# Regrouping a gather's 128 rows as 32 samples by 4 fields, and collecting all results for one turn at the end of a factorization-machine kernel

## The chip, the cores and the metric

The kernel runs on one core of a Trainium2 chip. The metric is the device time of that core in microseconds (us). Each core has TensorE (PE, matmul), VectorE (DVE), ScalarE (ACT), GpSimd (POOL), SyncE (SP), which here only issues transfers, and 16 DMA engines that move data between HBM and the on-chip memories SBUF and PSUM, both of 128 partitions.

## The reference, cut to what matters

For 2048 samples with 32 fields each, every field has its own table of 1250 rows of 496 floats. A sample picks one row of every table; the rows are scaled by the sample's values, and a factorization-machine term and a small hidden layer give one number per sample.

```python
gathered = jax.vmap(lambda table, idx: table[idx], in_axes=(0, 1), out_axes=1)(emb, xi)
e = gathered * xv[:, :, None]                  # 2048 x 32 x 496
s = jnp.sum(e, axis=1)
qi = 0.5 * (s * s - jnp.sum(e * e, axis=1))
h = jax.nn.relu(xv @ W1 + b1)                  # 2048 x 1024
x = jnp.concatenate([qi, h], axis=1)
return x @ W2 + b2                             # 2048 x 1
```

All data are float32. The gathered rows are 2048 x 32 x 1984 bytes, 130 MB.

## The kernel before, in words

**Tiling.** The samples go in 16 blocks of 128. A block is 8 quads, a quad is 4 gathers, and a gather is one indirect DMA that POOL issues: it brings 128 rows, one for each partition, from the addresses in one column of `index_rows` in SBUF (line 142). There are 16 x 8 x 4 = 512 gathers. The buffer `gathered` holds the 8 quads of one block, so quad s of block i goes where quad s of block i-1 was.

**Before**, the 128 partitions of a gather are 4 samples by 32 fields.

**For each quad**, in a stream that runs over all blocks: ACT squares the rows of two gathers at a time into PSUM (`squares`, line 160); DVE multiplies each of the four squared tiles by the weights `w2_all` and sums along the row (line 271, with a sum output into `norms`); PE multiplies the gathered rows by `weights`, a matrix that holds the samples' values in the right columns, and adds them up over the 8 quads in `sum_ps` (line 189). In quad 2 of a block PE also computes the hidden layer (line 202), which DVE weighs after quad 4 (line 283). After quad 3, DVE fills `weights` for the next block (line 233).

**At a block's end** ACT squares the sums (`sum_squared`, line 166), and DVE scales the norms by the squared values (line 288), spreads them over the samples' columns (line 293), weighs the squared sums (line 300), adds three partial results (line 305); PE adds the spread norms over partitions (line 176), and DVE adds that to the rest, after quad 1 of the next block (`finish`, line 241). After the last block PE turns the 128 x 16 results with an identity matrix (line 209), DVE copies them out of PSUM (line 310) and SP stores them.

**What sets the order.** Each engine works through its own list in the order written, and waits on semaphores. POOL waits ahead of each quad from block 1 on, until ACT has squared and PE has summed what the quad's buffer held (`squared`, `summed`). Row addresses are computed by DVE from the raw indices (`rows_of`, lines 222, 224 and 227), first for block 0 alone, then for the other 15 blocks together while the first gathers are issued.

Of the kernel before, what the change touches and what calls it, by code (L numbers as in the profile page):

```python
# [5 lines left out]
ALU = mybir.AluOpType  # L6
# [4 lines left out]
P = 128  # L11
# [4 lines left out]
def fm_kernel(nc, index, value, value_t, emb, w1, b1, w2, b2, out):  # L16


    fields, batch = value_t.shape
# [3 lines left out]
    per = P // fields  # L23
    blocks = batch // P
    quads = P // (GROUPS * per)
# [5 lines left out]
    assert per * quads == COLS and gathers == blocks * in_block and dim <= 512  # L31

    with ExitStack() as ctx:  # L33
# [11 lines left out]
        index_rows = sb("index_rows", [P, gathers], I32)  # L45
        values = sb("values", [P, 2, gathers])
        first_row = sb("first_row", [P, 1])
        last_row = sb("last_row", [P, 1])
        own_row = sb("own_row", [P, per])
        ones = sb("ones", [P, 1])  # L50

        weights = sb("weights", [P, 2, quads, GROUPS, COLS])
        gathered = sb("gathered", [P, quads, GROUPS, dim])

        weighted = sb("weighted", [P, GROUPS + halves + 1, 512])
        w2_all = sb("w2_all", [P, dim + hidden])
        w1_b1 = sb("w1_b1", [fields + 1, hidden])
        value_rows = sb("value_rows", [fields + 1, batch])
        sum_squared = sb("sum_squared", [P, 512])

        norms = sb("norms", [P, quads, GROUPS])
        norms_scaled = sb("norms_scaled", [P, quads, GROUPS])
        norms_spread = sb("norms_spread", [P, GROUPS, quads, per])
        parts = sb("parts", [P, 2 + halves])
        partial = sb("partial", [P, 1])
        y = sb("y", [P, blocks])

        column_less_row = sb("column_less_row", [P, P])
        identity = sb("identity", [P, P])
        y_rows = sb("y_rows", [blocks, P])  # L70
# [5 lines left out]
        norm_ps = psum("norm_ps", [P, 512])  # L76
# [19 lines left out]
        scaled = sem("scaled")  # L96
        spread_ready = sem("spread_ready")
        norm_ready = sem("norm_ready")
        partial_ready = sem("partial_ready")
        y_ready = sem("y_ready")  # L100
        identity_ready = sem("identity_ready")
        y_turned = sem("y_turned")
        y_rows_ready = sem("y_rows_ready")
# [5 lines left out]
        def _(sp):  # L109
# [6 lines left out]
            sp.dma_start(parts[:, 1 + halves:], b2.to_broadcast([P, 1])).then_inc(w2_loaded, 16)  # L116

            sp.wait_ge(y_rows_ready, 1)
            sp.dma_start(out.rearrange("(c p) o -> c (p o)", p=P), y_rows[:]).then_inc(stored, 16)
# [3 lines left out]
        def _(pool):  # L123
            for b in range(per):
                nc.gpsimd.iota(first_row[b * fields:(b + 1) * fields, :], [[0, 1]], base=0,
                               channel_multiplier=vocab,
                               allow_small_or_imprecise_dtypes=True).then_inc(rows_known, 1)
            pool.wait_ge(rows_known, per)
            nc.gpsimd.iota(column_less_row[:], [[1, P]], base=0, channel_multiplier=-1,
                           allow_small_or_imprecise_dtypes=True).then_inc(rows_known, 1)  # L130
            for i in range(blocks):
# [16 lines left out]
        def _(act):  # L148
            act.dma_start(w1_b1[0:fields, :], w1).then_inc(w1_loaded, 16)
            act.dma_start(w1_b1[fields:fields + 1, :], b1).then_inc(w1_loaded, 16)  # L150
            act.dma_start(value_rows[0:fields, :], value_t).then_inc(w1_loaded, 16)
            for i in range(blocks):
                for s in range(quads):
                    for half in range(pairs):
                        pair = slice(pairs * half, pairs * half + pairs)
                        act.wait_ge(fetched[s][half], (i + 1) * pair_arrived)
                        if i + s > 0:

                            act.wait_ge(normed, (i * quads + s - 1) * GROUPS + pairs * (half + 1))
# [4 lines left out]
                if i > 0:  # L164
                    act.wait_ge(sum_squared_used, i)
# [178 lines left out]
```

## Time and profile before

| | |
|---|---|
| time, median of 3 runs | 659.15 us (658.28 to 659.45) |
| the profiled execution, its own time | 656.74 us |
| its span, first to last instruction | 654.9 us |
| POOL busy | 485.8 us, 74% |
| DVE busy | 384.4 us, 59% |
| PE busy | 308.0 us, 47% |
| ACT busy | 265.8 us, 41% |
| data moved | 132.08 MB, mean 202 GB/s |

Busy time is the time in which an engine ran instructions. POOL's instructions here are the gathers: an entry is the time that POOL spends on issuing one, and between two entries there is always a gap that the profile calls "issue", in which nothing that it sees is waited for. In a timeline row the first number is the start from the span's start, the second how long it took, and the brackets tell how long the engine had been idle and for what. A DVE operation with a sum output shows a second entry for reading the sum (DVE_READ_ACCUMULATOR). DVE overlaps the end of one operation with the start of the next, so the next one can start some 0.08 us before the reported end.

### The profile page before, as it was taken

Reading aid. Unit: us, or ns where it says so; the run is one execution under the profiler, and the core shown is the slowest. Engines: PE = TensorE matmul, PEld = TensorE weight load, DVE = VectorE, ACT = ScalarE, POOL = GpSimd, SP = SyncE. Lnnn points to the kernel's source line nnn. Section 1 sums busy time; section 2 is a strip of 40 time slices with the busy share of each in tenths; the row PEclk is TensorE's granted clock in tenths of the full one; section 3 lists DMA queues with packets and bytes.
Section 4 is the critical chain, followed back from the end, with each engine's and each line's share of the span. In section 5 each row is a group of like instructions: output and inputs, shape, how many; then the busy total and the mean of one; then the engine's idle time right before and its main releaser. Section 6 shows DMA issues by size and latency. Waiting matters only on the chain.

```text
span 654.9 us, 4973 instructions
## 1 busy us (share of the span) xinstructions
PE 308.0 (47%) x1122; PEld 55.9 (9%) x1122; DVE 384.4 (59%) x1330; ACT 265.8 (41%) x273; POOL 485.8 (74%) x521
## 2 busy tenths in 40 slices
PE   1544536354453643546346353453635445364354
PEld 0101001010010100101001010100101001010010
DVE  6556655656666465655556555665555665556554
ACT  2344444434443434344343434444344444343433
POOL 5777777777777777777777777777777777777773
DMA  7777777777777777777777777777777777777774
GB/s 218 203 205 203 203 205 204 203 203 203 203 204 204 203 204 202 207 201 204 204 203 205 204 203 203 203 206 204 203 204 202 204 203 205 205 203 202 204 202 114
DMA packets 33647, 132.08 MB, mean 202 GB/s; under 512 B 8577, under 2 KB 8721, under 8 KB 33586
## 3 DMA queue, kind: packets, MB, share of 16 engines
q0 software_dynamic: 32768, 130.06, 72.4%
q1 hardware_dynamic: 752, 1.31, 0.7%
q10 hardware_dynamic: 98, 0.40, 0.2%
q8 instruction: 9, 0.15, 0.1%
q14 instruction: 20, 0.16, 0.1%
HBM read 131.72 MB, written 0.01 MB: 201 GB/s over the span
## 4 chain that ended last, share of the span: by engine, by line
POOL 60%; issue 20%; PE 10%; DMA 8%; DVE 1%; POOLq 0%; ACT 0%; DVEq 0%
POOL gathered L142 60%; DMA gathered<-emb,index_rows 7%; PE sum_ps L189 6%; PE hidden_ps L202 5%; DMA index_raw<-index 0%; POOLq L139 0%; DVE weighted L271 0%; POOLq L33 0%; ACT squares L160 0%; DVE weighted L300 0%; PE norm_ps L209 0%; DVE index_rows L227 0%; DVE y_rows L310 0%; DVE index_wrap L224 0%; DVE norms_scaled L288 0%
## 5 line engine op out<-in xcount | busy, mean ns | idle before, releaser
L142 POOL DMA_INDIRECT gathered<-emb,index_rows x512 | 484.8, 947 | 158.8 <-issue 151.1
L271 DVE SCALAR_TENSOR_TENSOR weighted<-squares,w_all 128x496 f32<-128x496 f32 x512 | 324.6, 672 | 261.3 <-ACT squares L160 261.0
L160 ACT ACTIVATE squares<-gathered 128x992 f32<-128x992 f32 x256 | 256.3, 1001 | 366.2 <-DMA gathered<-emb,index_rows 343.1
L189 PE MATMUL sum_ps<-gathered,weights 128*32 128x496 f32 x1024 | 240.8, 1031 | 343.4 <-DMA gathered<-emb,index_rows 343.4
L189 PEld LDWEIGHTS sum_ps<-gathered,weights 128*32 128x32 f32 x1024 | 29.0, 140 | 526.8 <-issue 526.8
L202 PE MATMUL hidden_ps<-w_b,value_rows 33*128 33x512 f32 x64 | 60.5, 1097 | 0.0
L271 DVE DVE_READ_ACCUMULATOR weighted<-squares,w_all 128x1 f32 x512 | 42.4, 83 | 0.0
L202 PEld LDWEIGHTS hidden_ps<-w_b,value_rows 33*128 33x128 f32 x64 | 18.6, 321 | 42.4 <-issue 42.4
L283 DVE SCALAR_TENSOR_TENSOR weighted<-hidden_ps,w_all 128x512 f32<-128x512 f32 x32 | 20.7, 686 | 0.0
L166 ACT ACTIVATE sum_squared<-sum_ps 128x496 f32<-128x496 f32 x16 | 9.3, 583 | 16.8 <-PE sum_ps L189 16.8
L233 DVE TENSOR_TENSOR weights<-values,own_row 128x16 f32<-128x16 f32 x128 | 12.7, 170 | 0.0
L300 DVE SCALAR_TENSOR_TENSOR weighted<-sum_squared,w_all 128x496 f32<-128x496 f32 x16 | 10.7, 666 | 0.0
L176 PEld LDWEIGHTS norm_ps<-ones,norms_spread 128*128 128x128 f32 x32 | 8.0, 313 | 26.8 <-issue 24.2
L176 PE MATMUL norm_ps<-ones,norms_spread 128*128 128x1 f32 x32 | 9.4, 363 | 0.9 <-DVE norms_spread L293 0.9
L293 DVE TENSOR_TENSOR norms_spread<-norms_scaled,own_row 128x128 f32<-128x128 f32 x16 | 4.8, 298 | 0.5
L288 DVE TENSOR_TENSOR norms_scaled<-norms,values 128x32 f32<-128x32 f32 x16 | 3.1, 192 | 0.6
L305 DVE TENSOR_REDUCE partial<-parts 128x1 f32<-128x4 f32 x16 | 2.5, 157 | 0.6
L283 DVE DVE_READ_ACCUMULATOR weighted<-hidden_ps,w_all 128x1 f32 x32 | 2.7, 83 | 0.0
L241 DVE TENSOR_TENSOR y<-partial,norm_ps 128x1 f32<-128x1 f32 x16 | 2.4, 151 | 0.0
L160 ACT ACT_TABLE_LOAD x1 | 1.3, 1283 | 2.1 <-issue 2.1
L263 DVE MEMSET value_rows<- 1x2048 f32 x1 | 1.8, 1765 | 0.5 <-ACT squares L160 0.5
L248 DVE MEMSET weights<- 128x2048 f32 x1 | 1.8, 1765 | 0.4 <-issue 0.4
(19 smaller groups left out, 7.3 us busy)
## 6 DMA issues: line engine op xcount, KB each, us to landing
gathered<-emb,index_rows POOLq DMA_INDIRECT x512, 3.7
w_all<-w SPq DMA_DIRECT2D x1, 760.0 KB, 6.1
values<-value SPq DMA_DIRECT2D x1, 256.0 KB, 3.5
value_rows<-value_t ACTq DMA_DIRECT2D x1, 256.0 KB
index_raw<-index SPq DMA_DIRECT2D x1, 240.0 KB, 4.7
w_b<-w ACTq DMA_DIRECT2D x1, 128.0 KB
index_raw<-index SPq DMA_DIRECT2D x1, 16.0 KB, 3.0
w_b<-b ACTq DMA_DIRECT2D x1, 4.0 KB
```

What stands on the lines that cost most here:

```text
L142: nc.gpsimd.indirect_dma_start(out=gathered[:, s, j, :], out_offset=None, in_=emb, in_offset=bass.IndirectOffsetOnAxis(ap=index_rows[:, g: ...
L160: nc.scalar.activation(squares[:, pair, 0:dim], gathered[:, s, pair], ACT.Square).then_inc(squared, 1)
L166: nc.scalar.activation(sum_squared[:, 0:dim], sum_ps[:, 0:dim], ACT.Square).then_inc(sum_squared_ready, 1)
L176: nc.tensor.matmul(norm_ps[:, 0:1], norms_spread[:], ones[:], start=True, stop=True).then_inc(norm_ready, 1)
L189: last = nc.tensor.matmul(sum_ps[j * COLS:(j + 1) * COLS, 0:dim], weights[:, i % 2, s, j, :], gathered[:, s, j, :], start=(s == 0), stop=( ...
L202: last = nc.tensor.matmul(hidden_ps[:, h, :], value_rows[:, i * P:(i + 1) * P], w1_b1[:, h * 512:(h + 1) * 512], start=True, stop=True)
L233: last = nc.vector.tensor_tensor(weights[:, i % 2, s, :, s * per:(s + 1) * per], values[:, 0, at].unsqueeze(2).to_broadcast([P, GROUPS, per]),
L271: nc.vector.scalar_tensor_tensor(weighted[:, j, 0:dim], squares[:, j, 0:dim], -0.5, w2_all[:, 0:dim], ALU.mult, ALU.mult, accum_out=norms[ ...
L283: nc.vector.scalar_tensor_tensor(weighted[:, GROUPS + h, :], hidden_ps[:, h, :], 0.0, w2_all[:, dim + h * 512:dim + (h + 1) * 512], ALU.ma ...
L288: nc.vector.tensor_tensor(norms_scaled[:].rearrange("p s j -> p (s j)"), norms[:].rearrange("p s j -> p (s j)"), values[:, 1, i * in_block ...
L293: nc.vector.tensor_tensor(norms_spread[:], norms_scaled[:].rearrange("p s j -> p j s").unsqueeze(3).to_broadcast([P, GROUPS, quads, per]), ...
L300: nc.vector.scalar_tensor_tensor(weighted[:, GROUPS + halves, 0:dim], sum_squared[:, 0:dim], 0.5, w2_all[:, 0:dim], ALU.mult, ALU.mult, ac ...
```

## The change

- A gather holds 32 samples by 4 fields in place of 4 samples by 32 fields. The weights of PE's matmul are then a mask of 32 columns times the values, filled by one DVE operation for each block; the mask is kept in PSUM (`y_ps`, columns 128 to 159).
- The norms are multiplied by the values at once: line 271's constant -0.5 becomes a scalar read from `values` for each partition (line 305 of the new kernel). The scaling, the spreading, the partial sum and the per-block matmul go away.
- The results of all blocks are kept (`norms`, `hidden_part`, `sum_part`) and turned at the very end by three matmuls with a 0/1 mask (`add_lines`).
- The weighing of the squared sums moves from a block's end to after quad 1 of the next block (`weigh_sums`), ACT's squaring of the sums to after quad 0 of the next block (`square_sums`), and the two halves of the hidden layer are weighed by one operation.
- `normed` is counted once a quad, `summed` once in two quads. POOL waits once in two quads, on `summed` alone; PE waits on `squared` in place of the transfers themselves, save in the last quad, so that `summed` implies both.
- The row addresses are computed with constants and a 128 x 32 table of first rows, and the 128 x 2048 memset of `weights` goes away.

The core of the diff:

```diff
-            for b in range(per):
-                nc.gpsimd.iota(first_row[b * fields:(b + 1) * fields, :], [[0, 1]], base=0,
-                               channel_multiplier=vocab,
+            for f in range(per):
+                nc.gpsimd.iota(first_row[f * COLS:(f + 1) * COLS, :], [[per * vocab, quads], [0, GROUPS]],
+                               base=f * vocab, channel_multiplier=0,
                                allow_small_or_imprecise_dtypes=True).then_inc(rows_known, 1)
...
-                    if i > 0:
-
-                        pool.wait_ge(squared, ((i - 1) * quads + s + 1) * pairs)
-                        pool.wait_ge(summed, (i - 1) * quads + s + 1)
+                    if i > 0 and s % freed == 0:
+
+                        pool.wait_ge(summed, (i - 1) * in_summed + s // freed + 1)
...
+            def square_sums(i):
+                act.wait_ge(summed, (i + 1) * in_summed)
+                if i > 0:
+                    act.wait_ge(sum_squared_used, i)
+                nc.scalar.activation(sum_squared[:], sum_ps[:, 0:dim],
+                                     ACT.Square).then_inc(sum_squared_ready, 1)
...
+                    if i + s > 0:
+
+                        act.wait_ge(normed, i * quads + s)
...
-                        if i + s > 0:
-
-                            act.wait_ge(normed, (i * quads + s - 1) * GROUPS + pairs * (half + 1))
...
+                    if s == 0 and i > 0:
+                        square_sums(i - 1)
+            square_sums(blocks - 1)
...
-                    for half in range(pairs):
-                        pe.wait_ge(fetched[s][half], (i + 1) * pair_arrived)
+                    if i == blocks - 1 and s == quads - 1:
+                        for half in range(pairs):
+                            pe.wait_ge(fetched[s][half], (i + 1) * pair_arrived)
+                    else:
+
+                        pe.wait_ge(squared, (i * quads + s + 1) * pairs)
...
+            def add_lines(part, first, last):
+
+                return nc.tensor.matmul(y_ps[0:lines, 0:COLS], part[:].rearrange("p i j -> p (i j)"),
+                                        own_sample[:], start=first, stop=last)
...
             def refill_weights(i):
-                for s in range(quads):
-                    at = slice(i * in_block + s * GROUPS, i * in_block + (s + 1) * GROUPS)
-                    last = nc.vector.tensor_tensor(
-                        weights[:, i % 2, s, :, s * per:(s + 1) * per],
-                        values[:, 0, at].unsqueeze(2).to_broadcast([P, GROUPS, per]),
-                        own_row[:].unsqueeze(1).to_broadcast([P, GROUPS, per]), ALU.mult)
-                last.then_inc(weights_ready, 1)
...
+                nc.vector.scalar_tensor_tensor(
+                    weights[:, i % 2],
+                    values[:, 0, i * in_block:(i + 1) * in_block].unsqueeze(2).to_broadcast(
+                        [P, in_block, COLS]), 1.0,
+                    y_ps[:, P:P + COLS].unsqueeze(1).to_broadcast([P, in_block, COLS]),
+                    ALU.mult, ALU.mult).then_inc(weights_ready, 1)
+
+            def weigh_sums(i):
+                dve.wait_ge(sum_squared_ready, i + 1)
+                nc.vector.scalar_tensor_tensor(
+                    weighted[:, GROUPS], sum_squared[:], 0.5, w2_all[:, 0:dim], ALU.mult, ALU.mult,
+                    accum_out=sum_part[:, i:i + 1]).then_inc(sum_squared_used, 1)
...
-                        nc.vector.scalar_tensor_tensor(
-                            weighted[:, j, 0:dim], squares[:, j, 0:dim], -0.5, w2_all[:, 0:dim],
-                            ALU.mult, ALU.mult, accum_out=norms[:, s, j:j + 1]).then_inc(normed, 1)
+                        last = nc.vector.scalar_tensor_tensor(
+                            weighted[:, j], squares[:, j, 0:dim], values[:, 1, g:g + 1],
+                            w2_all[:, 0:dim], ALU.mult, ALU.mult,
+                            accum_out=norms[:, i, s, j:j + 1])
+                    last.then_inc(normed, 1)
                     if s == 1 and i > 0:
-                        finish(i - 1)
+                        weigh_sums(i - 1)
...
+            add_quads(blocks - 1, blocks).then_inc(norm_lines_ready, 1)
+            weigh_sums(blocks - 1)
+            dve.wait_ge(sum_squared_used, blocks)
+            by_line(sum_part, sum_lines, blocks - 1, blocks).then_inc(sum_lines_ready, 1)
+            dve.wait_ge(y_summed, 1)
+            nc.vector.tensor_scalar(y[:], y_ps[0:lines, 0:COLS], b2_all[0:lines, :], None, ALU.add
+                                    ).then_inc(y_ready, 1)
```

How the change moves instructions is seen in each engine's list. A row gives the line, the operation, what it writes and reads, its shape and what it waits for; "x7" is seven such in a row.

On DVE, at quads 0 and 1 of block 1, the list of before has the addition of `finish` (line 241) behind the last squared tile of quad 1:

```order
L271 SCALAR_TENSOR_TENSOR weighted,norms<-squares,w_all 128x496 [waits squared]
L271 SCALAR_TENSOR_TENSOR weighted,norms<-squares,w_all 128x496
L241 TENSOR_TENSOR y<-partial,norm_ps 128x1 [waits norm_ready]
L271 SCALAR_TENSOR_TENSOR weighted,norms<-squares,w_all 128x496 [waits squared]
L271 SCALAR_TENSOR_TENSOR weighted,norms<-squares,w_all 128x496
```

The changed kernel has at the same place:

```order
L305 SCALAR_TENSOR_TENSOR weighted,norms<-squares,values,w_all 128x496 [waits squared]
L305 SCALAR_TENSOR_TENSOR weighted,norms<-squares,values,w_all 128x496
L262 SCALAR_TENSOR_TENSOR weighted,sum_part<-sum_squared,w_all 128x496 [waits sum_squared_ready]
L305 SCALAR_TENSOR_TENSOR weighted,norms<-squares,values,w_all 128x496 [waits squared]
L305 SCALAR_TENSOR_TENSOR weighted,norms<-squares,values,w_all 128x496
```

A small addition has been replaced by the weighing of 496 squared sums, which reads `sum_squared` and `w2_all`, both in SBUF.

On POOL, the list of before from the first row tables to the first quads of block 1 is:

```order
L125 IOTA first_row 32x1 x4
L129 IOTA column_less_row 128x128 [waits rows_known]
L142 DMA gathered<-emb,index_rows 128x496 [waits index_ready]
L142 DMA gathered<-emb,index_rows 128x496 x31
L142 DMA gathered<-emb,index_rows 128x496 [waits summed,squared,index_ready]
L142 DMA gathered<-emb,index_rows 128x496 x3
L142 DMA gathered<-emb,index_rows 128x496 [waits summed,squared]
```

The changed kernel's POOL list there is:

```order
L132 IOTA first_row 32x32 x4
L137 IOTA column_less_row 32x32 [waits rows_known]
L137 IOTA column_less_row 32x32 x3
L150 DMA gathered<-emb,index_rows 128x496 [waits index_ready]
L150 DMA gathered<-emb,index_rows 128x496 x31
L150 DMA gathered<-emb,index_rows 128x496 [waits summed,index_ready]
L150 DMA gathered<-emb,index_rows 128x496 x7
L150 DMA gathered<-emb,index_rows 128x496 [waits summed]
```

The number of gathers is the same; a wait stands ahead of every eighth instead of every fourth, and is for one semaphore.

On DVE, the list of before begins with the address operations and the fills of `weights`:

```order
L222 TENSOR_SCALAR index_wrap<-index_raw 128x32 [waits first_loaded,setup]
L224 SCALAR_TENSOR_TENSOR index_wrap<-index_wrap,first_row,index_raw 128x32 [waits setup]
L227 TENSOR_SCALAR index_rows<-index_wrap,first_row,last_row 128x32 [waits setup]
L248 MEMSET weights 128x2048
...
L233 TENSOR_TENSOR weights<-values,own_row 128x4x4 [waits values_loaded,setup]
L233 TENSOR_TENSOR weights<-values,own_row 128x4x4 x7
L256 TENSOR_TENSOR values<-values 128x512
L222 TENSOR_SCALAR index_wrap<-index_raw 128x480 [waits index_loaded,setup]
L224 SCALAR_TENSOR_TENSOR index_wrap<-index_wrap,first_row,index_raw 128x480 [waits setup]
L227 TENSOR_SCALAR index_rows<-index_wrap,first_row,last_row 128x480 [waits setup]
```

The changed kernel's list begins so:

```order
L241 TENSOR_SCALAR index_wrap<-index_raw 128x32 [waits first_loaded,rows_known]
L243 SCALAR_TENSOR_TENSOR index_wrap<-index_raw,index_wrap 128x32 [waits setup]
L246 SCALAR_TENSOR_TENSOR index_rows<-index_wrap,first_row 128x32 [waits setup]
L282 TENSOR_SCALAR own_sample<-column_less_row 128x32 [waits rows_known]
L283 TENSOR_SCALAR y_ps<-column_less_row 128x32
L253 SCALAR_TENSOR_TENSOR weights<-values,y_ps 128x1024 [waits values_loaded,setup]
L287 SCALAR_TENSOR_TENSOR values<-values 128x512
L241 TENSOR_SCALAR index_wrap<-index_raw 128x480 [waits index_loaded,setup]
L243 SCALAR_TENSOR_TENSOR index_wrap<-index_raw,index_wrap 128x480 [waits setup]
L246 SCALAR_TENSOR_TENSOR index_rows<-index_wrap,first_row 128x480 [waits setup]
```

The memset and the eight small fills have given way to two comparisons and one fill of 1024 elements; of the three address operations the third reads two tensors now.

## Rows read from the trace of the kernel before

**Rows 1.** The page: busy shares, and the costliest group of instructions.

```profile
PE 308.0 (47%) x1122; PEld 55.9 (9%) x1122; DVE 384.4 (59%) x1330; ACT 265.8 (41%) x273; POOL 485.8 (74%) x521
...
L142 POOL DMA_INDIRECT gathered<-emb,index_rows x512 | 484.8, 947 | 158.8 <-issue 151.1
```

**Rows 2.** Timeline of DVE and POOL at the start.

```profile
4.09 0.25 DVE L224 SCALAR_TENSOR_TENSOR index_wrap<-index_wrap,first_row,index_raw 128x32 f32<-128x32 f32 x1
4.38 0.30 DVE L227 TENSOR_SCALAR index_rows<-index_wrap,first_row,last_row 128x32 int32<-128x32 f32 x1
4.97 1.09 POOL L142 DMA_INDIRECT gathered<-emb,index_rows  x1 [3.12 <-DVE index_rows L227]
...
8.00 0.68 DVE L256 TENSOR_TENSOR values<-values 128x512 f32<-128x512 f32 x1
8.72 0.41 DVE L222 TENSOR_SCALAR index_wrap<-index_raw 128x480 f32<-128x480 int32 x1
8.87 1.08 POOL L142 DMA_INDIRECT gathered<-emb,index_rows  x1 [0.30 <-issue]
...
10.25 1.01 POOL L142 DMA_INDIRECT gathered<-emb,index_rows  x1 [0.30 <-issue]
```

**Rows 3.** Timeline: the last gather, and what ACT and DVE do last.

```profile
644.51 0.95 POOL L142 DMA_INDIRECT gathered<-emb,index_rows  x1 [0.30 <-issue]
...
650.29 0.58 ACT L166 ACTIVATE sum_squared<-sum_ps 128x496 f32<-128x496 f32 x1 [1.05 <-PE sum_ps L189]
...
651.02 0.67 DVE L300 SCALAR_TENSOR_TENSOR weighted<-sum_squared,w_all 128x496 f32<-128x496 f32 x1
...
651.73 0.16 DVE L305 TENSOR_REDUCE partial<-parts 128x1 f32<-128x4 f32 x1
651.92 0.15 DVE L241 TENSOR_TENSOR y<-partial,norm_ps 128x1 f32<-128x1 f32 x1
...
652.84 0.28 DVE L310 COPY y_rows<-norm_ps 16x128 f32<-16x128 f32 x1 [0.77 <-PE norm_ps L209]
```

**Rows 4.** Waits on POOL, 10.2 to 45 us: us in total, times, longest.

```profile
POOL gathered L142 <- issue: 8.5, 28, 0.3
```

**Rows 5.** Waits on POOL, 45 to 640 us.

```profile
POOL gathered L142 <- issue: 140.7, 462, 0.3
POOL gathered L142 <- PE sum_ps L189: 4.6, 15, 0.3
```

**Rows 6.** Timeline of DVE and POOL, late in block 11 to 12.

```profile
490.34 0.67 DVE L271 SCALAR_TENSOR_TENSOR weighted<-squares,w_all 128x496 f32<-128x496 f32 x1
...
490.71 0.95 POOL L142 DMA_INDIRECT gathered<-emb,index_rows  x1 [0.30 <-PE sum_ps L189]
...
491.48 0.67 DVE L300 SCALAR_TENSOR_TENSOR weighted<-sum_squared,w_all 128x496 f32<-128x496 f32 x1
491.97 1.00 POOL L142 DMA_INDIRECT gathered<-emb,index_rows  x1 [0.30 <-issue]
```

**Rows 7.** Timeline of DVE and POOL at the end of another block.

```profile
130.38 0.29 DVE L293 TENSOR_TENSOR norms_spread<-norms_scaled,own_row 128x128 f32<-128x128 f32 x1
130.44 1.04 POOL L142 DMA_INDIRECT gathered<-emb,index_rows  x1 [0.30 <-issue]
```

**Rows 8.** Timeline of DVE and POOL at the end of a third block.

```profile
411.38 0.67 DVE L300 SCALAR_TENSOR_TENSOR weighted<-sum_squared,w_all 128x496 f32<-128x496 f32 x1
411.94 0.95 POOL L142 DMA_INDIRECT gathered<-emb,index_rows  x1 [0.30 <-issue]
```

**Rows 9.** Groups of DVE by line, whole span: busy, mean ns of one.

```profile
L288 DVE TENSOR_TENSOR norms_scaled<-norms,values 128x32 f32<-128x32 f32 x16 | 3.1, 192 | 0.6
```

**Rows 10.** Timeline: the first of the 15 `finish` additions between blocks.

```profile
60.02 0.15 DVE L241 TENSOR_TENSOR y<-partial,norm_ps 128x1 f32<-128x1 f32 x1
60.35 0.95 POOL L142 DMA_INDIRECT gathered<-emb,index_rows  x1 [0.30 <-issue]
```

**Rows 11.** Timeline: the fourteenth of them.

```profile
580.55 0.15 DVE L241 TENSOR_TENSOR y<-partial,norm_ps 128x1 f32<-128x1 f32 x1
...
580.76 0.95 POOL L142 DMA_INDIRECT gathered<-emb,index_rows  x1 [0.30 <-issue]
```

**Rows 12.** Line 142, whole span: from a gather's issue to its landing.

```profile
DMA to landing us min/median/max: 3.4/3.7/5.5
```

More of the change, by code:

```diff
@@ L22, in fm_kernel @@
     hidden = w1.shape[1]
[L23 removed]
+    per = P // COLS
     blocks = batch // P
[L25 removed]
+    quads = fields // per
     gathers = index.shape[1]
@@ L30, in fm_kernel @@
     pair_arrived = 16 * GROUPS // pairs
-    assert per * quads == COLS and gathers == blocks * in_block and dim <= 512
+    freed = 2
+    in_summed = quads // freed
+    lines = blocks * GROUPS
+    assert per * quads == fields and gathers == blocks * in_block and dim <= 512
+    assert lines <= P and halves == 2
     with ExitStack() as ctx:
@@ L219, in step, with rows_of @@
                 dve.wait_ge(setup, done[0])
-            def rows_of(columns):
+            def rows_of(first, last):
+                columns = slice(first * in_block, last * in_block)
+                by_block = [P, last - first, in_block]
                 step(nc.vector.tensor_scalar(index_wrap[:, columns], index_raw[:, columns], 0.0,
@@ new lines, in by_line, with add_quads @@
+            def by_line(part, lines_of, first, last):
+                count = [P, last - first, GROUPS]
+                return nc.vector.tensor_tensor(
+                    lines_of[:, first:last], part[:, first:last].unsqueeze(2).to_broadcast(count),
+                    own_group[:].unsqueeze(1).to_broadcast(count), ALU.mult)
+            def add_quads(first, last):
+                return nc.vector.tensor_reduce(
+                    norm_lines[:, first:last], norms[:, first:last].rearrange("p i s j -> p i j s"),
+                    mybir.AxisListType.X, ALU.add)
@@ L244, in _ @@
             dve.wait_ge(rows_known, per)
-            step(nc.vector.tensor_scalar(last_row[:], first_row[:], float(vocab - 1), None, ALU.add))
             dve.wait_ge(first_loaded, 16)
-            rows_of(slice(0, in_block))
-            nc.vector.memset(weights[:], 0.0)
-            nc.vector.memset(ones[:], 1.0)
-            step(nc.vector.memset(own_row[:], 0.0))
-            for b in range(per):
-                last = nc.vector.memset(own_row[b * fields:(b + 1) * fields, b:b + 1], 1.0)
@@ L257, in _ @@
             dve.wait_ge(index_loaded, 16)
-            rows_of(slice(in_block, gathers))
-            dve.wait_ge(rows_known, per + 1)
-            nc.vector.tensor_scalar(identity[:], column_less_row[:], 0.0, None, ALU.is_equal
-                                    ).then_inc(identity_ready, 1)
+            rows_of(1, blocks)
+            step(nc.vector.memset(own_group[:], 0.0))
+            for j in range(GROUPS):
+                last = nc.vector.memset(own_group[j * COLS:(j + 1) * COLS, j:j + 1], 1.0)
@@ L262, in _ @@
+            step(last)
             dve.wait_ge(w1_loaded, 48)
@@ new lines, in _ @@
+                    if i == blocks - 1 and s == 5:
+                        dve.wait_ge(hidden_used, blocks)
+                        by_line(hidden_part, hidden_lines, 0, blocks).then_inc(hidden_lines_ready, 1)
+                        dve.wait_ge(sum_squared_used, blocks - 1)
+                        by_line(sum_part, sum_lines, 0, blocks - 1)
+                        dve.wait_ge(normed, (blocks - 1) * quads)
+                        add_quads(0, blocks - 1)
+            dve.wait_ge(normed, blocks * quads)
```

159 lines of the change are left out of this document (65 added, 94 removed).

## The prediction, as put on record

> **What bounds the kernel now.** I read the page first. POOL is the busiest engine, and all of it is one group: 512 gathers of 947 ns, with 151 us of "issue" gaps between them [rows 1]. One gather so costs 0.95 + 0.30 = 1.25 us from start to start. From the first start at 4.97 us [rows 2] to the last at 644.51 us [rows 3] there are 511 steps in 639.5 us, 1.2516 us each. The list of POOL's waits shows that it never waits for anybody in earnest: the 28 gathers of block 0 that have no buffer to wait for had 8.5 us of gaps, 0.304 us each [rows 4]; later 462 gaps total 140.7 us, 0.305 us each, and the 15 that the profile lays to PE total 4.6 us, 0.307 us each [rows 5]. So the kernel is a metronome of 512 beats, with 5 us ahead of it and 654.9 - 644.5 = 10.4 us behind the last beat. An engine other than POOL matters only if it makes POOL miss a beat, or in those two ends. 0.2% is 1.3 us, or 2.6 ns a beat.
>
> What can disturb a beat shows in the timeline. A beat's entry is 0.95 us long almost always. At 491.97 it is 1.00, and a DVE operation that reads two SBUF tensors (line 300, `sum_squared` and `w2_all`) had started at 491.48 and was still running, its reported end 0.18 us past the beat's start [rows 6]. At 130.44 it is 1.04: line 293, also with two SBUF inputs, ends 0.23 us past the start [rows 7]. At 8.87 it is 1.08: line 222 ends 0.26 us past it; it reads one tensor, but two elements at a time (480 in 0.41 us, against 0.68 us for line 256's 512) [rows 2]. At 411.94 it is the usual 0.95 with line 300 ending 0.11 us past it [rows 8]. All four fit one rule: **a beat that begins while such an operation runs is late by the operation's reported end minus the beat's start minus 0.13 us** (0.05, 0.10, 0.13 and 0). Line 271, which reads one tensor in PSUM and one in SBUF, runs across a beat's start 243 times, as at 490.34 to 491.01 over the start at 490.71, and delays none: 0.95 [rows 6]. Late beats are never made up, as POOL has no slack.
>
> The Trainium skill (SBUF — State Buffer, "Who interferes with whom") says that a DVE instruction with two SBUF inputs shares a read interface with a GpSimd instruction that reads SBUF, and that the second to come blocks until the first is done. The trace agrees in kind; its four delays are shorter, by 0.13 us, than the operation's remaining time. The same page ("A bandwidth-pool intuition that's wrong") reports blocking until DVE's end and some 115 ns more; by that, term c below would be 13 x 0.245 = 3.2 us more (an estimate from that page), and the trace's 1.00 in place of some 1.25 at 491.97 speaks against it.
>
> **The change part by part.**
>
> a) *Waits on POOL.* Before, 120 pairs of waits; after, 60 single ones. Gaps with and without waits differ by 0.001 to 0.003 us [rows 4, 5], so 60 to 180 waits removed are worth from nothing to 180 x 0.003 = 0.5 us. I take 0: the gaps are alike within the rounding. The new wait comes later, for PE's second quad of a pair, which itself waits for ACT. Quad 1 of block 1 is issued by 55 us, landed by 59 us, squared by 60 us and summed by 62 us, and POOL asks for it ahead of beat 64, at 4.97 + 64 x 1.2516 = 85 us. 20 us of cover; cost 0. If that cover were gone, all that stands behind POOL's wait, which is every later gather, would slip.
>
> b) *Start.* The first beat follows the third address operation. Lines 224 and 227 take 0.25 and 0.30 us, each with per-partition scalars as well as tensors [rows 2]. Their replacements have no such scalar; the nearest row is a two-input operation of the same 32 elements, 0.19 us [rows 9]. That is 0.06 + 0.11 = **-0.17**; bounds 0 and -0.2. POOL's iotas grow but are done before the indices land. Next come collisions: before, the beats at 8.87 and 10.25 lost 0.13 and 0.06 us [rows 2]. After, `values` is squared and the addresses of 15 blocks computed some 2 us sooner, and three operations of the latter's kind have two SBUF inputs, each about 0.7 us (line 256, 0.68 us [rows 2]). They fill 2.0 of some 3 us, so one or two beats start under one and lose between 0 and 0.68 - 0.13 = 0.55 us each: 0 to 1.1 us, I take 0.5, net of before **+0.3**.
>
> c) *The weighing of the squared sums*, 0.67 us with two SBUF inputs. Before, at a block's end, it happened to start mostly just behind a beat. After, it starts where line 241 starts now, right behind the last tile of quad 1, 15 times. That place is 0.33 us ahead of a beat the first time [rows 10] and 0.21 us the fourteenth [rows 11]; over the 15 the distances are 0.33, 0.26, 0.96, 0.33, 0.25, 0.55, 0.37, 0.27, 0.37, 0.32, 0.50, 0.40, 0.26, 0.21 and 1.01 us. An operation of 0.67 us that starts d ahead of a beat delays it by 0.67 - d - 0.13 = 0.54 - d. Summed over the twelve where it is positive: **2.6 us**. The chain to this place is tied to the beat: landing 3.7 us behind the issue [rows 12], 1.0 us of ACT, two DVE operations. The only thing that moves it is those two operations, which gain a per-partition scalar. No row prices that for them: at most the 0.25 - 0.19 = 0.06 us by which line 224 exceeds line 288 [rows 2, 9], at least nothing, as starts of DVE operations overlap. Two such shift the place by 0 to 0.12 us toward the beat, which gives 2.6 to 4.2 us over the 15. I take the middle, 0.06 us later: **+3.4**.
>
> d) *Collisions removed.* Lines 293 and 300 go from the block's end. Four beats lost 0.31 us there in all, the largest two of them in [rows 6, 7] (0.05 and 0.10), the others 0.08 each: **-0.3**. The eight fills of line 233 cost no beat today; their one successor reads only one SBUF tensor, and hides behind the beats.
>
> e) *Steady work of DVE, ACT and PE.* DVE is 59% busy [rows 1] and loses more than it gains; ACT now waits for a whole quad to be weighed: 1.0 us of ACT and four times 0.6 us of DVE is 3.5 us for a quad, against four beats, 5.0 us. **0.** Without that slack every quad would cost the difference.
>
> f) *Tail.* The sums are ready on ACT at 650.87, the weighing starts at 651.02 behind lines 288 and 293 [rows 3]; after, one short reduction stands there, and it starts at about 650.93: -0.09. Behind it, a reduction and an addition (651.73 and 651.92) become one operation: -0.19. The matmul stays; the copy of 128 elements (0.28 us) becomes one of 32: -0.08. The store goes out as 64 pieces of 128 bytes in place of 16 of 512: from 0 to, at most, what is saved; I take +0.1. Sum **-0.26**.
>
> Sum: -0.17 + 0.3 + 3.4 - 0.3 - 0.26 = **+3.0 us** on the profiled execution's 656.74. The median of the runs is 659.15; the same gives **662.1 us**, +0.45%. What a measurement of this kernel can tell from no change is 0.2%, 1.3 us.
>
> **The rivals.**
>
> 1. *Not slower.* The sum operation lies clear of the beats: if the new arrangement of rows makes transfers land 0.2 us sooner, it ends before the beat, and if some 0.35 us later, it starts behind one. Then c is near 0 and the rest is -0.17 + 0.3 - 0.3 - 0.26 = -0.4: 658.7 us, no change. For it: landings scatter from 3.4 to 5.5 us [rows 12], two of the 15 places lie clear already. Against: thirteen of 15 distances are 0.21 to 0.55 us, so the median is stable, and the rows are as long and as scattered as before. It decides where c is below 1.7 us, which a place 0.1 us farther ahead of the beat gives (1.5 us). Chance 0.22.
>
> 2. *Faster.* As 1, with the start's collisions also missed and the waits worth their 0.5 us: -0.17 - 0.2 - 0.3 - 0.26 - 0.5 = -1.4 us, 657.7 us. All the small savings must come in together. Chance 0.07.
>
> 3. *Full blocking.* Each of the 13 beats under 0.67 us away waits for the operation's whole rest, 0.13 us more: +1.7, 663.8 us. The four rows above speak against it, but they are short overlaps. Chance 0.12.
>
> 4. *The per-partition scalar makes line 305 block POOL as well.* It is read from SBUF like `w2_all`. By the rule above, applied to each run of line 271 across a beat, that is 62 us: 721 us. Against it: nothing in the trace tells, since the scalar operations there have two tensors anyway or stand alone. Chance 0.03. The Trainium skill (DVE: scalar operands, raw-bit mode, write accounting and state across instructions, "Scalar operands") says that such a scalar does not take up the second tensor stream, which no run here shows yet.
>
> **How the numbers follow.** The forecast, c between 1.5 and 5 us, has 0.56, its own range 660.3 to 663.6. With the rivals 1, 2, 3 and 4 (0.22, 0.07, 0.12, 0.03) that is one. Slower by over 0.2%: 0.56 + 0.12 + 0.03, less a little for the forecast's low edge, 0.68; same 0.24; faster 0.08. The range from 658.5 to 664.3 leaves out rival 4, rival 2 and the edges of 1 and 3.
>
> **What would show it.** In the changed kernel's timeline: 512 beats of 0.95 us, gap 0.30 with and without waits (a); first beat at 4.80 us (b); in 10 to 14 of the 15 blocks one beat of 1.1 to 1.4 us, with line 262 started 0.1 to 0.5 us before it (c); no long beats elsewhere but at the start (d), and none under line 305 (rival 4); from the last beat to the end 10.1 us in place of 10.4 (f). I am wrong if line 262 runs across beats that stay at 0.95 us, if it starts elsewhere in the beat, or if the steady gap itself has changed by some ns.

## The result and the profile after

The changed kernel took 661.28 us (median of 7 runs, 661.20 to 661.48), the kernel before 658.61 us on the same chip (7 runs, the first three included). The ratio is 1.0038 (95% interval 1.0026 to 1.0049): 2.7 us slower, clear of the 0.2% that this measurement can tell. The forecast was 3.0 us.

The page of the changed kernel has, against [rows 1]:

```profile
PE 300.4 (46%) x1094; PEld 45.7 (7%) x1094; DVE 410.0 (62%) x1125; ACT 265.8 (40%) x273; POOL 491.5 (75%) x524
...
L150 POOL DMA_INDIRECT gathered<-emb,index_rows x512 | 489.9, 957 | 157.6 <-issue 155.8
L305 DVE SCALAR_TENSOR_TENSOR weighted<-squares,values,w_all 128x496 f32<-128x496 f32 x512 | 355.5, 732 | 242.0 <-ACT squares L176 241.6
```

POOL still sets the pace. Its 512 gathers are busy 5.1 us longer in sum (484.8 in rows 1, 489.9 here) with the same gaps. DVE's tile operation grew from 672 to 732 ns; what is new in it is the per-partition scalar (the third experiment takes it away again).

The timeline of the changed kernel's DVE and POOL where the squared sums of block 0 are weighed, against [rows 10] (start, duration, idle time before; a "beat" is one gather's issue, as in the prediction):

```profile
59.09 0.73 DVE L305 SCALAR_TENSOR_TENSOR weighted<-squares,values,w_all 128x496 f32<-128x496 f32 x1
...
59.75 0.67 DVE L262 SCALAR_TENSOR_TENSOR weighted<-sum_squared,w_all 128x496 f32<-128x496 f32 x1
...
60.01 1.23 POOL L150 DMA_INDIRECT gathered<-emb,index_rows  x1 [0.30 <-issue]
...
61.54 0.95 POOL L150 DMA_INDIRECT gathered<-emb,index_rows  x1 [0.30 <-issue]
```

Line 262 starts 0.26 us ahead of the beat at 60.01 and its reported end is 0.41 us past it; the beat takes 1.23 in place of 0.95 us: 0.41 - 0.13 = 0.28. The next beat follows 1.53 us behind. Line 305, which runs across the beats beside it, leaves them at 0.95. Three other blocks, in which the distance differs:

```profile
222.54 0.67 DVE L262 SCALAR_TENSOR_TENSOR weighted<-sum_squared,w_all 128x496 f32<-128x496 f32 x1
...
223.02 1.02 POOL L150 DMA_INDIRECT gathered<-emb,index_rows  x1 [0.30 <-issue]
...
303.04 0.67 DVE L262 SCALAR_TENSOR_TENSOR weighted<-sum_squared,w_all 128x496 f32<-128x496 f32 x1
...
303.65 0.94 POOL L150 DMA_INDIRECT gathered<-emb,index_rows  x1 [0.30 <-issue]
...
624.91 0.67 DVE L262 SCALAR_TENSOR_TENSOR weighted<-sum_squared,w_all 128x496 f32<-128x496 f32 x1
...
625.06 1.35 POOL L150 DMA_INDIRECT gathered<-emb,index_rows  x1 [0.30 <-issue]
```

At 0.48 us of distance the beat loses 0.07 us, at 0.61 nothing, at 0.15 us 0.40. Of the 15 places 14 have such a late beat; their start-to-start times exceed 1.25 us by 3.93 us together, and each by its operation's reported end minus the beat's start minus 0.13 us, to 0.01 us.

The start of the changed kernel, against [rows 2]:

```profile
3.75 0.19 DVE L243 SCALAR_TENSOR_TENSOR index_wrap<-index_raw,index_wrap 128x32 f32<-128x32 int32 x1
3.97 0.19 DVE L246 SCALAR_TENSOR_TENSOR index_rows<-index_wrap,first_row 128x32 int32<-128x32 f32 x1
...
4.44 1.10 POOL L150 DMA_INDIRECT gathered<-emb,index_rows  x1 [1.79 <-DVE index_rows L246]
...
5.53 0.68 DVE L287 SCALAR_TENSOR_TENSOR values<-values 128x512 f32<-128x512 f32 x1
5.84 1.19 POOL L150 DMA_INDIRECT gathered<-emb,index_rows  x1 [0.30 <-issue]
```

From the second address operation to the first beat it is 0.69 us in place of 0.88 (4.09 to 4.97): 0.19 us saved, with operations of 0.19 us each. One beat, at 5.84, starts under an operation with two SBUF tensors and takes 0.24 us more.

The tail, against [rows 3]:

```profile
649.28 0.95 POOL L150 DMA_INDIRECT gathered<-emb,index_rows  x1 [0.31 <-issue]
...
655.05 0.58 ACT L165 ACTIVATE sum_squared<-sum_ps 128x496 f32<-128x496 f32 x1 [1.05 <-PE sum_ps L198]
...
655.67 0.68 DVE L262 SCALAR_TENSOR_TENSOR weighted<-sum_squared,w_all 128x496 f32<-128x496 f32 x1
...
656.38 0.16 DVE L269 TENSOR_TENSOR sum_lines<-sum_part,own_group 128x4 f32<-128x4 f32 x1
...
657.06 0.24 DVE L338 TENSOR_SCALAR y<-y_ps,b_all 64x32 f32<-64x32 f32 x1 [0.52 <-PE y_ps L218]
657.33 0.53 SPq L126 DMA_DIRECT2D out<-y  x1
```

The last beat starts 10.16 us ahead of the span's end (10.2 by the rounded 659.4), against 10.41 before.

**A part of the two traces' difference is not the change's.** The spans differ by 4.5 us, the medians by 2.7. The changed kernel's profile is of an execution at its median (661.24), that of before one of 656.74, 1.9 us under the median of before (658.61). The beats that nothing disturbs (start to start below 1.27 us) average 1.2503 us before and 1.2535 us after; 494 of them make 1.6 us. The first and the fifth run below settle whose that is.

### The profile page after: what moved, and what is told of

Its sections match the earlier page's. It is cut to its first block, busy times and chain, and to the rows that moved or that the text cites. A ratio compares the mean times of both kernels' runs of the same rounds, so it can differ in the third digit from the quotient of the medians.

```text
span 659.4 us, 4310 instructions
## 1 busy us (share of the span) xinstructions
PE 300.4 (46%) x1094; PEld 45.7 (7%) x1094; DVE 410.0 (62%) x1125; ACT 265.8 (40%) x273; POOL 491.5 (75%) x524
## 4 chain that ended last, share of the span: by engine, by line
POOL 74%; issue 24%; DMA 1%; DVE 1%; POOLq 0%; ACT 0%; PE 0%; DVEq 0%
POOL gathered L150 74%; DMA gathered<-emb,index_rows 1%; DMA index_raw<-index 0%; DVE weighted L305 0%; POOLq L39 0%; ACT squares L176 0%; DVE weighted L262 0%; PE y_ps L218 0%; DVE y L338 0%; DVE norm_lines L274 0%; DVE index_rows L246 0%; DVE index_wrap L243 0%; DVE index_wrap L241 0%; DVE sum_lines L269 0%; DVEq L279 0%
## 5 line engine op out<-in xcount | busy, mean ns | idle before, releaser
L150 POOL DMA_INDIRECT gathered<-emb,index_rows x512 | 489.9, 957 | 157.6 <-issue 155.8
L305 DVE SCALAR_TENSOR_TENSOR weighted<-squares,values,w_all 128x496 f32<-128x496 f32 x512 | 355.5, 732 | 242.0 <-ACT squares L176 241.6
L198 PEld LDWEIGHTS sum_ps<-gathered,weights 128*32 128x32 f32 x1024 | 26.2, 140 | 566.1 <-ACT squares L176 468.8
L305 DVE DVE_READ_ACCUMULATOR weighted<-squares,values,w_all 128x1 f32 x512 | 42.5, 83 | 0.0
L319 DVE SCALAR_TENSOR_TENSOR weighted_hidden<-hidden_ps,w_all 128x1024 f32<-128x1024 f32 x16 | 19.5, 1220 | 0.0
L253 DVE SCALAR_TENSOR_TENSOR weights<-values,y_ps 128x1024 f32<-128x1024 f32 x16 | 19.5, 1217 | 0.0
```

The source lines that it names most:

```text
L150: nc.gpsimd.indirect_dma_start(out=gathered[:, s, j, :], out_offset=None, in_=emb, in_offset=bass.IndirectOffsetOnAxis(ap=index_rows[:, g: ...
L198: last = nc.tensor.matmul(sum_ps[j * COLS:(j + 1) * COLS, 0:dim], weights[:, i % 2, s * GROUPS + j, :], gathered[:, s, j, :], start=(s == ...
L253: nc.vector.scalar_tensor_tensor(weights[:, i % 2], values[:, 0, i * in_block:(i + 1) * in_block].unsqueeze(2).to_broadcast([P, in_block, ...
L305: last = nc.vector.scalar_tensor_tensor(weighted[:, j], squares[:, j, 0:dim], values[:, 1, g:g + 1], w2_all[:, 0:dim], ALU.mult, ALU.mult, ...
L319: nc.vector.scalar_tensor_tensor(weighted_hidden[:], hidden_ps[:], 0.0, w2_all[:, dim:].rearrange("p (h c) -> p h c", h=halves), ALU.max, ...
```

## The experiments

Each ratio is to the kernel before, run beside it on the same chip; its 95% interval stands in brackets. Before took 656.79 us (19 runs) beside the first four kernels and 657.33 us (14 runs) beside the others. The theory is the prediction's: a beat that starts while DVE runs an operation with two SBUF tensors is late, and the change puts one such operation ahead of a beat in each block. The rivals are that the time comes from the regrouped rows, from the waits, or from another feature of the place behind quad 1.

**Before again**, no edit.

> The kernel before, once more, for its profile. The first trace of before had an undisturbed beat (start to start of two gathers) of 1.2503 us, the changed kernel's 1.2535 us, 1.6 us over 494 beats. If that difference is one execution against another, this profile shows a beat of 1.2530 to 1.2540 us and a span near 657 us; if it comes from the change (the regrouped rows, the waits), it shows 1.2500 to 1.2506 us again.

It took 657.06 us, span 655.2. The undisturbed beat was 1.2503 us, as in the first trace. That left the changed kernel's 1.2535 open, which the fifth run took up. It also showed a rarer collision at the old place, here in the timeline of DVE and POOL:

```profile
210.29 0.67 DVE L300 SCALAR_TENSOR_TENSOR weighted<-sum_squared,w_all 128x496 f32<-128x496 f32 x1
210.33 1.45 POOL L142 DMA_INDIRECT gathered<-emb,index_rows  x1 [0.30 <-issue]
```

Line 300 began 0.04 us ahead of a beat, so its end is 0.63 us past it, and the beat is 0.50 us too long: the same rule at the longest overlap of a late beat in any trace here. The same trace shows where the rule ends, at another block:

```profile
611.22 0.72 DVE L300 SCALAR_TENSOR_TENSOR weighted<-sum_squared,w_all 128x496 f32<-128x496 f32 x1
611.24 0.95 POOL L142 DMA_INDIRECT gathered<-emb,index_rows  x1 [0.30 <-issue]
```

Here line 300 began 0.02 us ahead of the beat. By the rule the beat would be late by 0.57 us; it is on time, and it is DVE's operation that is longer, 0.72 us in place of 0.67. The traces have eleven beats of this kind, behind operations with two SBUF tensors that began 0.00 to 0.04 us ahead of them; every late beat has a lead of 0.04 us or more. In this execution lines 293 and 300 took 0.85 us from the beats, against 0.31 in the first trace. The kernel before is not free of the effect; it mostly just misses it.

**The sums in PSUM.** The operation stays, at its place and in its order, and has one SBUF input in place of two.

```diff
-                nc.scalar.activation(sum_squared[:], sum_ps[:, 0:dim],
+                nc.scalar.activation(sum_ps[:, 0:dim], sum_ps[:, 0:dim],
...
-                    weighted[:, GROUPS], sum_squared[:], 0.5, w2_all[:, 0:dim], ALU.mult, ALU.mult,
+                    weighted[:, GROUPS], sum_ps[:, 0:dim], 0.5, w2_all[:, 0:dim], ALU.mult, ALU.mult,
...
-                        pe.wait_ge(sum_squared_ready, i)
+                        pe.wait_ge(sum_squared_used, i)
```

> The changed kernel, but ACT squares the sums in place in PSUM, and line 262 reads them there: at the same place in the same order, with one SBUF tensor in place of two. Theory (beats that start under a two-SBUF operation are late): the 14 long beats of 1.02 to 1.35 us go away, 3.9 us less, 657.4 us, 0.998 of before. Rival (the time comes from the regrouped rows or from what else is on DVE at that place): the beats stay long and the time stays at 661.3 us, 1.004 of before.

655.73 us, ratio 0.998 (0.997 to 0.999): faster than both kernels. The timeline at the same place of block 1:

```profile
59.81 0.67 DVE L262 SCALAR_TENSOR_TENSOR weighted<-sum_ps,w_all 128x496 f32<-128x496 f32 x1
60.11 0.95 POOL L150 DMA_INDIRECT gathered<-emb,index_rows  x1 [0.31 <-issue]
```

Line 262 starts 0.30 us ahead of the beat (0.26 us in the changed kernel), is as long as there, and the beat is 0.95 us. No beat after the second is late in the whole execution, though in all 15 blocks line 262 starts 0.14 to 0.45 us ahead of one. So it is the second SBUF input, and not the place, its length or what is near it. The undisturbed beat is 1.2501 us, with the regrouped rows and the new waits.

**The constant in place of the per-partition scalar** (this leaves out the scaling of the norms by the values).

```diff
-                            weighted[:, j], squares[:, j, 0:dim], values[:, 1, g:g + 1],
+                            weighted[:, j], squares[:, j, 0:dim], -0.5,
```

> The changed kernel with the constant -0.5 in line 305 in place of the per-partition scalar, so the norms are left unscaled by the values. Each tile's operation should be 0.67 us long again in place of 0.73, and the place of the weighing lies 0.12 us farther ahead of the beat. Theory: the long beats lose 0.12 us each, 14 x 0.12 = 1.6 us less, 659.7 us, 1.0017 of before. Rival (the scalar costs nothing here, or blocks POOL by itself): no change, 661.3 us, or many us less with shorter beats under line 305.

657.83 us, ratio 1.0015 (1.0006 to 1.0024), within 0.0002 of the forecast. The groups of DVE by line show the operation back at its old length:

```profile
L305 DVE SCALAR_TENSOR_TENSOR weighted<-squares,w_all 128x496 f32<-128x496 f32 x512 | 325.0, 672 | 268.7 <-ACT squares L176 267.5
```

Eleven beats are late, by 1.92 us together, as their distances are longer: 0.40 us on average in place of 0.29, over the places less than 0.7 us ahead of a beat (the first happens to move by more, from 0.26 to 0.50 us). The scalar costs nothing under a beat, and 60 ns an operation on DVE, which bring the weighing 0.11 us nearer to the beat; 0.12 was expected.

**Only the move, in the kernel before.** Lines 300 and 305 go behind quad 1 of the next block; `weigh` holds the eight lines word for word.

```diff
                     if s == 1 and i > 0:
+                        weigh(i - 1)
                         finish(i - 1)
...
-                dve.wait_ge(sum_squared_ready, i + 1)
-                nc.vector.scalar_tensor_tensor(
-                    weighted[:, GROUPS + halves, 0:dim], sum_squared[:, 0:dim], 0.5, w2_all[:, 0:dim],
...
```

> The kernel before with one thing changed: the weighing of the squared sums and the sum of the parts (lines 300 and 305) go from a block's end to behind quad 1 of the next block, ahead of finish. Theory: 12 to 14 beats are late by 0.54 us minus the distance, 2.6 us in all, and the 0.05 of line 300 at the old place goes away: 661.1 us against 658.6, 1.0039. Rival (the move alone is harmless and the changed kernel's time comes from its other parts): 658.6 us, 1.000.

659.97 us, ratio 1.004 (1.0026 to 1.0053). The old kernel with this one move is as slow as the whole change, but not for one reason alone. Its 14 late beats at the new place lose 2.50 us, against 2.6 worked out from the first trace's distances; that is most of the 3.2 us by which its median exceeds that of before, and the fills below give about 1.0 us of late beats more. The longest, in its timeline:

```profile
623.45 0.67 DVE L247 SCALAR_TENSOR_TENSOR weighted<-sum_squared,w_all 128x496 f32<-128x496 f32 x1
623.53 1.40 POOL L142 DMA_INDIRECT gathered<-emb,index_rows  x1 [0.30 <-PE sum_ps L189]
```

Not expected were nine beats under the eight small fills of `weights` (line 233), late by 0.97 us together. In the first trace of before only one was late by 0.02 us or more, in its second two, by 0.14 us together. The fills have two SBUF inputs, are 0.17 us long each and start 0.09 us apart. A beat starts among the fills in every block of both kernels, so it isn't that they meet more beats here; the rule for single operations does not give these delays, and why they are longer here was not tried.

**The changed kernel again**, no edit.

> The changed kernel once more. Its first trace had an undisturbed beat of 1.2535 us; the four profiles since, three of them of variants of before or of the changed kernel, had 1.2500 to 1.2503. If the 3 ns belong to the chip or the execution, this profile shows 1.2500 to 1.2503 us, 13 or 14 long beats, 3.5 to 4.2 us lost in them, and a ratio to before of 1.003 to 1.005, with a span 1.5 us shorter than the first's. If they belong to the changed kernel, the beat is 1.2535 again.

659.41 us, ratio 1.0035 (1.0021 to 1.0048), span 657.3. The undisturbed beat is 1.2499 us. The groups of line 150, min/median/max of a gather in ns, first in the changed kernel's first trace and then in this one:

```profile
L150 POOL DMA_INDIRECT gathered<-emb,index_rows x512: 945/949/1347, 4.4 to 649.3; - x171
```

```profile
L150 POOL DMA_INDIRECT gathered<-emb,index_rows x512: 942/946/1366, 4.6 to 647.1; - x171
```

So the 3 ns belonged to the chip or the execution, and not to the change. Twelve beats were late, by 3.42 us together: one beat and 0.1 us less than the least that was expected.

**Three weighings.** Two more operations of the same form in each of 14 blocks (their result is not used), with `idle` set to zero at the start.

```diff
                     if s == 1 and i > 0:
                         weigh_sums(i - 1)
+                    if s in (5, 7) and 0 < i < blocks - 1:
+                        nc.vector.scalar_tensor_tensor(
+                            scratch[:], idle[:], 0.5, w2_all[:, 0:dim], ALU.mult, ALU.mult,
+                            accum_out=scratch_sum[:])
```

> The changed kernel, with an operation of the form of line 262 (two SBUF tensors, 128 x 496, result not used) added behind quads 5 and 7 of the 14 blocks 1 to 14, 28 in all. DVE has the time: it is 62% busy. Theory: each that starts 0 to 0.54 us ahead of a beat delays it by its reported end minus the beat's start minus 0.13 us, 0.28 us on average as the 14 of line 262 do, 28 x 0.28 = 7.8 us in all if they fall as those do, 669 us against 661.3, 1.016 of before; at least a third of it if they fall less well. Rival (only the place behind quad 1 is slow, for another reason): no more than 1 us, 1.006.

666.45 us, ratio 1.0139 (1.0124 to 1.0155), 7.0 us above the changed kernel. Of the 28 added operations 25 delay a beat, by 7.0 us together, 0.28 us each; if all 28 had, it would have been the 7.8 us of the forecast. The longest in the timeline:

```profile
253.37 0.67 DVE L317 SCALAR_TENSOR_TENSOR scratch<-idle,w_all 128x496 f32<-128x496 f32 x1
253.42 1.43 POOL L153 DMA_INDIRECT gathered<-emb,index_rows  x1 [0.30 <-issue]
```

DVE is busy 64% in this kernel, so its load does not explain it. The place behind quad 1 is nothing special.

**The waits of before.** `summed` is counted each quad, and POOL waits as before.

```diff
-    freed = 2
+    freed = 1
...
-                    if i > 0 and s % freed == 0:
+                    if i > 0:
 
+                        pool.wait_ge(squared, ((i - 1) * quads + s + 1) * pairs)
                         pool.wait_ge(summed, (i - 1) * in_summed + s // freed + 1)
```

> The changed kernel with POOL's waits of before: ahead of every quad, on squared and summed, and summed counted once a quad. Theory (a wait that is over costs POOL nothing, term a at 0): the beat stays at 1.250 us with the waits, 1.004 of before as the changed kernel. Rival (180 waits at 3 ns): 0.5 us more, 1.005; a wait that holds POOL's start by more shows in longer gaps at every fourth beat.

659.58 us, ratio 1.0035 (1.0021 to 1.0048): the same as the changed kernel beside it. The undisturbed beat is 1.2502 us against 1.2499; 496 of these make 0.15 us, and the 13 late beats at line 262's place (263 in this kernel) lose 4.08 us. A gain from fewer waits is below what can be told.

**The squaring of `values` on ACT**, on top of the sums in PSUM.

```diff
+            act.wait_ge(values_loaded, 16)
+            nc.scalar.activation(values[:, 1], values[:, 0], ACT.Square, scale=0.5 ** 0.5
+                                 ).then_inc(values_squared, 1)
...
-            step(nc.vector.scalar_tensor_tensor(values[:, 1], values[:, 0], -0.5, values[:, 0],
-                                                ALU.mult, ALU.mult))
...
-            add_lines(norm_lines, False, False)
+            add_lines(norm_lines, False, False, minus_sample)
```

> The variant with the sums in PSUM, and the squaring of values at the start moved from DVE (two SBUF inputs) to ACT, with the sign taken by a second mask in the last matmuls. Theory: the beat at 5.8 us that lost 0.24 to 0.31 us is undisturbed, 0.3 us less than the variant before it, 0.9975 of before. Rival (the start's lost time turns up at the next operation with two SBUF inputs, the address computation, which moves 0.7 us ahead): no gain, 0.998.

655.48 us, ratio 0.9974 (0.9964 to 0.9984). The second beat, in its timeline, is undisturbed:

```profile
5.91 0.95 POOL L152 DMA_INDIRECT gathered<-emb,index_rows  x1 [0.30 <-issue]
```

The address operations that follow do not make a beat late: the one at 6.64 us (0.66 us long) runs across the start of the beat at 7.16 us, overlapping it by 0.14 us, and the one at 7.33 us ends ahead of the next beat. Only the first of the 512 beats is still long (1.09 us), as in every kernel here. The advantage of this variant over the one with the sums in PSUM alone, 0.3 us in the traces, is inside both intervals. It has the lowest time of all: 1.85 us under before beside it and 3.9 us under the changed kernel.

## Why the prediction was right

**The sign and the mechanism** were right: the late beats of line 262 carry the loss. Three runs show it from three sides: taking away the second SBUF input takes the loss away, the move alone brings 14 such late beats and 2.5 us to the old kernel, and more such operations cost as much for each that meets a beat (25 of 28).

That the sum came so near is partly luck. By the first trace the terms are -0.19, +0.04, +3.93, -0.31 and -0.25, in all +3.2 us against the forecast's +3.0: the collisions at the start were put 0.26 us too high and the weighing 0.5 us too low, and these errors offset one another.

**a) Waits: 0.** Right, as the run with the waits of before shows.

**b) Start: -0.17 for the addresses.** Measured -0.19. **+0.3 for collisions**: mis-sized. One beat was late by 0.24 us, against 0.20 us in two beats before, so +0.04. The estimate took one or two of three operations to be hit; it was one, for less than its most, and a second was near. In the timeline of the changed kernel's first trace:

```profile
7.29 0.73 DVE L243 SCALAR_TENSOR_TENSOR index_wrap<-index_raw,index_wrap 128x480 f32<-128x480 int32 x1
7.33 0.94 POOL L150 DMA_INDIRECT gathered<-emb,index_rows  x1 [0.30 <-issue]
```

By the rule this beat would be 0.56 us late; with a lead of 0.04 us it is one of the eleven on time. The first beat also came earlier as its indices landed at 3.53 us in place of 3.87. In the first trace of before and in its second the first beat was at 4.97 and 4.78 us, in the changed kernel's two at 4.44 and 4.57. The landing differs by 0.1 to 0.2 us between executions of one kernel, so a good part of this need not be the change's; whether the rest is was not tried.

**c) +3.4 for the weighing.** 3.93 us in the first trace, 3.42 in the second, 4.08 with the waits of before. This is the term that was mis-sized, by 0.5 us in the first trace. The middle that was taken for the scalar (0.03 us an operation) was too low: it is 0.06, the upper bound, by which the term was worked out as 4.2. What brought the measured sums below that is that the distances scatter from execution to execution, and one to three of the 15 operations fall clear.

**d) -0.3 for the collisions removed.** This was read off one execution; in another it was 0.85 us. The term should have been a range up to 0.9; with the mean of the two, 0.6, the forecast would be the 2.7 us that were measured (2.1 us in the second comparison, on another chip), though two executions are few for a mean.

**e) Steady work: 0.** Right: in the changed kernel's first trace 269 beats start under line 305, and none is over 0.01 us longer than usual; the late ones, save the first of all, lie under an operation with two SBUF tensors.

**f) Tail: -0.26.** Measured -0.25 (10.41 to 10.16 us), but two of its parts were wrong and offset one another. The squared sums' weighing starts 0.11 us sooner, as forecast. From the reduction to the copy it is 0.68 us in place of 1.11 (656.38 to 657.06, against 651.73 to 652.84 in [rows 3]), 0.43 us less where the forecast had 0.19: the last matmuls, taken to stay as they were, keep the copy waiting for 0.52 in place of 0.77 us. And from the copy's end to the end of the span it is 2.14 us in place of 1.81: the store of 64 pieces costs 0.33 us more, not 0.1.

**The range.** With c between 1.5 and 5 us the terms give 660.2 to 663.7 us; the prediction has 660.3 to 663.6, a slip that changes nothing.

**The rivals.** Full blocking is refuted: the 125 late beats under a single operation with two SBUF tensors, in nine traces, obey the rule with the 0.13 us to 0.01 us, up to an overlap of 0.63 us. The figure of the Trainium skill (SBUF — State Buffer, "A bandwidth-pool intuition that's wrong"), blocked until DVE's end and some 115 ns, does not hold for these gathers: at an overlap of 0.63 us it would give 0.75 us (an estimate by that page); measured are 0.50. The scalar of line 305 blocks nothing, and that the weighing lies clear of the beats came true for one to three blocks of a trace only.

What stays open is which part of a gather's issue DVE's second read holds up, what decides at a lead of about 0.04 us which of the two waits, and why the small fills cost 1.0 us in one kernel and next to nothing in another.

## What to carry to other kernels

When POOL issues the transfers and sets the pace, look at DVE's operations for two tensors in SBUF, and at what lies under the start of each gather: 0.67 us of such an operation cost 0.28 us on average where a beat started under it, though DVE was busy for no more than 64% of the time. An operation that begins within 0.04 us ahead of the gather cost it nothing. Put one of the two tensors in PSUM, or give the work to ACT, as two runs did here. Moving the operation in program order only helps if its distance to the next gather is known. Read a collision's price from more than one execution, because the phases drift by some tenths of a microsecond.

## What the runs showed of the hardware

The granted TensorE clock fell in the two variants with the sums in PSUM, and in no other kernel. In the windows of the variant without the ACT squaring (length, busy time and number of instructions of PE, its weight loads, DVE, ACT and POOL, then the granted clock, the DMA share and GB/s):

```profile
20.00:60.00 40.00, 15.32 (x56) 2.37 (x52) 24.58 (x68) 16.50 (x17) 30.25 (x32) 1.00 0.73 203
60.00:100.00 40.00, 15.90 (x68) 2.72 (x68) 25.22 (x70) 16.50 (x17) 30.26 (x32) 0.60 0.72 203
100.00:300.00 200.00, 78.84 (x340) 13.59 (x340) 125.57 (x346) 82.47 (x85) 151.28 (x160) 0.55 0.73 204
```

PE there waits for the weighing at each block's start, and does not work for over 10 us each time (10.0 to 10.5 us, 15 times; in the changed kernel's first trace its longest pause, once the first gathers have landed, is 4.0 us). The first, in its timeline:

```profile
60.63 2.71 PE L198 MATMUL sum_ps<-gathered,weights 128*32 128x496 f32 x12 [10.23 <-DVE weighted L262]
```

From there on the mean granted clock is 0.55 to 0.60 of full speed, that is, much of the time the lower level of 1.2 GHz. These pauses are what sets the two variants apart from the others; that they are the cause of the lower clock was not tried by itself. It cost no beat, as PE is done with a buffer at least 20.8 us before POOL asks for it. What the lower clock would cost a kernel that PE bounds is not shown here.
